# Inverse deviation of four layer norms as exp of minus half a log, in one table set of ScalarE

## The reference, cut to what matters

```python
attn_out = ctx @ Wo.T + bo
x = hidden_states + attn_out
mu = jnp.mean(x, axis=-1, keepdims=True)
var = jnp.mean(jnp.square(x - mu), axis=-1, keepdims=True)
return (x - mu) / jnp.sqrt(var + 1e-05) * ln_g + ln_b
```

## Time and profile before

| what | before |
|---|---|
| median of 3 runs | 374.36 us (373.85 to 374.52) |
| profiled execution | 374.17 us |
| its span | 372.4 us |
| TensorE busy | 365.6 us, 98% of the span |
| VectorE busy | 217.8 us, 58% |
| ScalarE busy | 205.0 us, 55% |
| GpSimd busy | 123.8 us, 33% |

### The profile page before, as it was taken

How to read it: one execution, slowest core, us unless ns; L and a number is a source line. 1 busy time by engine, 2 the same in 40 slices (tenths; PEclk the granted TensorE clock), 3 DMA queues, 4 the chain that set the end, 5 groups by cost and what they waited for, 6 DMA issues and landing times.

```text
span 372.4 us, 6622 instructions
## 1 busy us (share of the span) xinstructions
PE 365.6 (98%) x2396; PEld 309.1 (83%) x2396; DVE 217.8 (58%) x363; ACT 205.0 (55%) x368; POOL 123.8 (33%) x125
## 2 busy tenths in 40 slices
PE   7999999999999999999999999999999999999996
PEld 4576898969878869787879899988988988989985
DVE  3946889897898867535667263343344434344334
ACT  2185357867569885475573665442843728166221
POOL 5068011430200724041072533441561445234500
PEclk9999999999999999999999999999999999999999
DMA  6993038107248117000000000000000000000004
GB/s 196 314 383 126 3 100 203 31 2 183 67 122 176 37 34 179 9 2 1 2 1 2 0 2 0 2 0 1 2 0 2 0 2 1 2 0 3 28 30 169
DMA packets 25057, 22.48 MB, mean 60 GB/s; under 512 B 9537, under 2 KB 20546, under 8 KB 25026
## 3 DMA queue, kind: packets, MB, share of 16 engines
q1 hardware_dynamic: 24352, 22.04, 21.1%
q10 hardware_dynamic: 674, 0.02, 0.1%
HBM read 12.35 MB, written 3.15 MB: 42 GB/s over the span
## 4 chain that ended last, share of the span: by engine, by line
PE 93%; SPq 3%; DMA 2%; issue 1%; DVE 0%; ACT 0%
PE slot L563 90%; SPq L495 2%; DMA xyz_n<-in_ctx 1%; DMA q_stack<-shiftT 1%; PE slot L683 1%; PE slot L724 1%; PE slot L692 1%; SPq L524 1%; PE slot L668 0%; DVE points L1333 0%; SPq L546 0%; PE slot L741 0%; SPq L447 0%; ACT low L881 0%; SPq L397 0%
## 5 line engine op out<-in xcount | busy, mean ns | idle before, releaser
L1080 POOL TENSOR_TENSOR p_lo<-p_full,p_hi 128x512 fp32r<-128x512 f32 x64 | 82.7, 1309 | 165.7 <-ACT p_full L1031 99.1
L1333 DVE SCALAR_TENSOR_TENSOR points<-slot,points 128x512 f32<-128x512 f32 x64 | 43.3, 689 | 65.6 <-PE slot L563 65.6
L1041 ACT ACTIVATE u_hi<-slot 128x512 fp32r<-128x512 f32 x64 | 36.9, 597 | 78.8 <-PE slot L563 78.7
L1328 DVE TENSOR_TENSOR u_lo<-slot,u_hi 128x512 fp32r<-128x512 f32 x64 | 42.9, 687 | 41.8 <-ACT u_hi L1041 41.7
L563 PE MATMUL slot<-adj,u_hi 128*128 128x512 f32 x256 | 66.0, 393 | 0.0
L563 PE MATMUL slot<-adj,u_lo 128*128 128x512 f32 x256 | 65.8, 391 | 0.0
L563 PE MATMUL slot<-fs_lo,p_hi 128*128 128x256 f32 x256 | 64.0, 283 | 0.0
L563 PE MATMUL slot<-fs_hi,p_hi 128*128 128x256 f32 x256 | 63.9, 283 | 0.0
L563 PEld LDWEIGHTS slot<-adj,u_lo 128*128 128x128 f32 x256 | 46.8, 188 | 9.1 <-DVE u_lo L1328 0.2
L563 PEld LDWEIGHTS slot<-adj,u_hi 128*128 128x128 f32 x256 | 46.0, 188 | 8.5
L563 PEld LDWEIGHTS slot<-fs_lo,p_hi 128*128 128x128 f32 x256 | 48.9, 191 | 0.6
(11 more groups left out here) (144 smaller groups left out, 552.4 us busy)
## 6 DMA issues: line engine op xcount, KB each, us to landing
q_stack<-q_hi SPq DMA_DIRECT2D x32, 128.0 KB, 2.4
x_in<-in_xT SPq DMA_DIRECT2D x8, 256.0 KB, 5.3
q_stack<-q_lo SPq DMA_DIRECT2D x16, 128.0 KB, 3.2
out_points<-points SPq DMA_DIRECT2D x8, 256.0 KB, 2.0
loraB_raw<-in_lora_BT SPq DMA_DIRECT2D x1, 1024.0 KB, 7.8
wk<-in_WkT SPq DMA_DIRECT2D x1, 1024.0 KB, 10.8
wq_raw<-in_WqT SPq DMA_DIRECT2D x1, 1024.0 KB, 10.5
wv<-in_WvT SPq DMA_DIRECT2D x1, 1024.0 KB, 11.4
```

What stands on the lines that cost most here:

```text
L1041: act.activation(half_of(u_hi[:, u], i % 2), bank("wa", b, i // 2, i % 2), ACT.Copy)\
L1080: pool.tensor_tensor(lo[:, cut], full[:, cut], hi[:, cut].bitcast(F32), ALU.subtract)\
L1328: dve.tensor_tensor(half_of(u_lo[:, u], i % 2), bank("wa", b, i // 2, i % 2), half_of(u_hi[:, u], i % 2).bitcast(F32), ALU.subtract).then_ ...
L1333: dve.scalar_tensor_tensor(pts, bank("ga", b, i // 2, i % 2), 1.0 / (TOPK + 1), pts, ALU.mult, ALU.add).then_inc(points_ready, 1)
```

## The change

The `dev` step on ScalarE takes the natural logarithm of variance plus `eps` in place of the square root, waits for that result itself (a new semaphore `act_step`), and takes the exponential of minus a half of it straight into `rstd`. The `ln` step on VectorE waits for `rstd_ready` and has no reciprocal any more. In front of ScalarE's steps, behind its three DMA issues, the program names the table set `natural_log_exp_and_others` to be loaded. The steps `rd`, `nm` and `pln`, which no order contains, are removed with their semaphores, their tile `to_norm` and the helper `wait_ln` (its callers wait for `ln_dve` directly, as they did). The five orders are the same.

```diff
@@ ScalarE, in front of its steps
             act.dma_start(rb_all[:], router_b.unsqueeze(0).broadcast_to([P, NE])).then_inc(loads["rb"], 16)
+            act.preload_act_table_set("natural_log_exp_and_others")
@@ ScalarE, step dev
                     after(act, var_ready, "st", b, 0)
                     after(act, var_ready, "st", b, 1)
-                    act.activation(dev[:, b], mean_var[:, b, :, 1], ACT.Sqrt, bias=eps[:]).then_inc(dev_ready, 1)
-                elif kind == "nm":
...
+                    act.activation(dev[:, b], mean_var[:, b, :, 1], ACT.Ln, bias=eps[:]).then_inc(act_step, 1)
+                    after(act, act_step, "dev", b)
+                    act.activation(rstd[:, b], dev[:, b], ACT.Exp, scale=-0.5).then_inc(rstd_ready, 1)
@@ ScalarE, steps ph and lk
                     if i < 2:
-                        wait_ln(act, b)
+                        after(act, ln_dve, "ln", b)
@@ VectorE, step ln
                 elif kind == "ln":
-                    after(dve, dev_ready, "dev", b)
-                    link(dve.reciprocal(rstd[:, b], dev[:, b]))
+                    after(dve, rstd_ready, "dev", b)
                     after(dve, centered, "ce", b, 0)
                     after(dve, centered, "ce", b, 1)
```

## The result

The changed kernel takes 376.71 us as the median (376.34 to 377.57), the kernel before 374.3 us beside it; the ratio is 1.0056 with a 95% interval of 1.0035 to 1.0078. It is slower by 0.6%, and I had forecast no change, at 374.3 us, with 374.9 as the upper end.

What follows compares the result with a forecast made beforehand. TensorE was taken to bound the kernel, 93% of the chain, with four waits, none behind a norm. All terms came to 0 on 374.17 us, about 374.2, put at 374.3 us; range 373.6 to 374.9 us.

Steps and rivals of the forecast that it cites:

- The table loads: ScalarE: three of four loads go, 4.1 us less work there with broken overlap, none of it seen at the end.
- The pair of logarithm and exponential: ScalarE's norms: logarithm, wait and exponential add 0.4 us per norm, 1.6 us for four, all covered.
- my two bounds: Handover from logarithm to exponential on ScalarE: between 0.03 and 0.12 us.
- The gain at norms 0 and 2 given back: ScalarE's queue comes 1.0 us earlier after each, lost again at its next wait for VectorE (0.42 and 1.36 us).
- The reciprocals: VectorE: four reciprocals go, 0.8 us less work there, nothing gained in the time.
- Rival 1: SyncE's issues before `shiftT` start earlier: 373.8 us, chance 0.10; with further short stalls won, 373.4 us, chance 0.07.
- its sign: The chain of SyncE issues before `shiftT` beginning before 136.2 us, named as showing the forecast wrong.
- Rival 2: Norm 1: the pair outlasts its cover, which decides from 0.88 us of added time; 375.0 us, chance 0.04.
- Rival 3: ScalarE: the one table set lacks a function, so loads alternate 15 times; 384 us, chance 0.04.
- the unused branches: Norm variants on GpSimd and ScalarE, with no step in the order: removing them costs nothing.
- The wait for `shiftT`: TensorE at 152 us waits for the DMA into `q_stack`: not released by ScalarE, stays at 0.5 us.
- the 0.03 of chance for a slower cause not seen: Whole kernel: chance 0.03 moved from same to slower for an unseen cause, within 0.09 for slower.

Runs made afterwards that it cites:

- e1: The changed kernel with an unused tile of 32 bytes per partition where `to_norm` was: 374.5 us, ratio 0.9997 to the kernel before.
- e10: The kernel before, old norms, without `to_norm` and with 32 unused bytes in front of `wq_hi` and `u_hi`: 373.8 us, ratio 0.9982.
- e12: The changed kernel with 32 unused bytes in place of `to_norm` and norm 1's logarithm-exponential pair taken four times in a row: 375.83 us, ratio 1.0026.
- e2: The kernel before with only the declaration of the unused tile `to_norm` taken away: 376.27 us, ratio 1.0063.
- e4: The changed kernel with 96 unused bytes in the place of `to_norm`: 375.99 us, ratio 1.0048.

## Why the prediction was wrong, point by point

- **The table loads: right.** One load is left, at the start, ahead of a wait for a DMA. ScalarE's busy time fell by 3.1 us to 201.9 (forecast 202.5; three loads are 3.85 us, four exponentials of 0.20 us take 0.8 back), and none of it came out at the end.
- **The pair of logarithm and exponential: mechanism right, size too large.** This is ScalarE of the changed kernel at norm 1 (compare):

```profile
126.39 0.30 ACT L978 ACTIVATE dev<-mean_var,eps 128x2 f32<-128x2 f32 x1 [0.60 <-DVE mean_var L1276]
126.72 0.20 ACT L980 ACTIVATE rstd<-dev 128x2 f32<-128x2 f32 x1
126.83 0.84 ACT L950 ACTIVATE v_blk<-v_rows 64x256 f32<-64x256 f32 x2
...
128.49 1.09 ACT L1025 ACTIVATE u_hi<-slot 128x512 fp32r<-128x512 f32 x2 [0.30 <-PE slot L553]
129.68 2.12 ACT L963 ACTIVATE probT<-slot,mask_col 128x1024 f32<-128x1024 f32 x2
```

  From the logarithm's start to the next instruction it is 0.44 us, where I had 0.6; the handover is 0.03 us, the lower of my two bounds, and the exponential takes 0.20. The addition is 0.24 us and not 0.4. The idle stretch before `u_hi` shrank from 0.54 to 0.30 us, by just that, and the copy stayed in time.
- **The gain at norms 0 and 2 given back: right.** The waits for VectorE at which it was to go grew, from 0.42 to 0.56 us and from 1.36 to 1.61 us, and e1 is at 0.9997 of the kernel before.
- **The reciprocals: right.** VectorE is busy for 0.8 us less, with four instructions less, and nothing came of it.
- **Rival 1, an earlier row of SyncE issues:** didn't happen, though its sign did. The row begins at 135.94 us in place of 136.30. But ScalarE's `dev` at norm 1 is already 0.42 us earlier (126.39 against 126.81), before any freed exponential, and e10, with the old norms and all their loads, begins the row at 135.75 us. The front of the program wanders by that much.
- **Rival 2, the cover at norm 1:** didn't happen; e12 shows that the point from which it decides lies where the sum put it.
- **Rival 3, functions missing in the set:** didn't happen, one load in all.
- **The step that failed** is half a sentence: that the unused branches "cost nothing by going". I looked for their instructions, of which there are none, and for their waits. I didn't ask what the declaration of their tile held in place. It is 32 bytes of room, and it kept `u_hi` on the same offset within 256 bytes as `adj`. Its going costs 1.5 us in the last 166 us and 0.3 us before that (the cost was put at nothing), and this is the loss that e2 shows alone and e1 undoes alone.
- **The wait for `shiftT`** was forecast to stay at 0.5 us and went to 1.3. Its chain of SyncE issues has one late issue:

```profile
137.77 1.75 SPq L514
...
148.76 3.75 DMA q_stack<-shiftT
```

  In the kernel before it is another one, and shorter:

```profile
140.53 1.19 SPq L495
```

  In the row of 18 issues from 136 us on, each of the fourteen profiled executions has exactly one of over 1 us (1.07 to 1.75), and each time it is one of four places. The wait goes with its length: 1.07 us and a wait of 0.2 in e1, 1.75 and 1.3 in the changed kernel. It came out between 0.2 us (e1) and 1.3 us (changed), at 1.2 us in e10, which has the old norms and is fast, and at 0.5 us in e4, which is slow. It follows neither the norms nor the addresses of `u`. What makes an issue late is open. I had treated this row as fixed, and it wanders by over 1 us; of the 2.4 us between the two profiled spans it is 0.8. e1, with the new norms and the old addresses, has no loss in its median, so the norms don't bring it; each kernel was profiled once, so what it is worth in the other medians is not shown.

The range was too narrow for this: its ends came from the waits alone, and nothing in it stood for a pace of TensorE that changes while no wait grows with it. Only the 0.03 of chance for a slower cause not seen covered it.

## What to carry to other kernels

A declaration that goes or comes is a change to every tile behind it. Where TensorE sets the time, compare the addresses of its weights and of its moving side before and after an edit, even if the edit removes only unused things, and keep how they lie to each other, as the room of e1 did (declaring the hot tiles first, or with their own alignment, should do it too; I didn't try it). When a kernel gets slower without a new wait, compare the length of a stretch of the same instructions in both chains, here 996 matmuls, before looking for a cause in the steps that were edited.

## What the runs showed of the hardware that I had not expected

- TensorE's fp32r matmuls with 128 x 128 weights and 512 moving columns follow each other at 229 ns when the tiles of weights and moving side begin at the same offset within 256 bytes, and at 233 ns when these differ, here by 32 (either way), 64 or 128 bytes. Eight kernels stand on the one side and six on the other (e12, with the addresses of the kernel before, has 164.67 us as well). The offsets rest on sizes rounded up to 32 bytes, as said. Matmuls of 256 columns don't show this slowing; with a difference of 32 bytes they follow at 118.2 to 118.4 ns, against 118.9 to 119.7 where the offsets agree.
- A logarithm and an exponential of 128x2 on ScalarE, each waiting for the one before, come at 0.56 us a pair, with 0.03 us from the end of one to the start of the next.
- Of the 121 DMA issues of SyncE, 8 to 11 take 1.0 to 2.7 us in every kernel, where the median is 0.6 us; in the row before `shiftT` it is one of 18, at a place that moves by a few issues.
